# Graph kernel with two gather layers: four row buffers instead of two, eight index buffers, and loops of more chunks

## What is computed

```
# layer 0
deg  = segment_sum(1, dst);  norm = rsqrt(deg[src]) * rsqrt(deg[dst])
x    = layernorm(x + segment_sum(x[src] * norm, dst))
# layer 1
h    = relu(edge_feat @ W1 + b1);  w = (h @ W2 + b2).reshape(e, 4, 8, 8)
m0   = ALPHA * ((s[src] * sh0) . w_000 + C110 * (v[src] * sh1) . w_110)
m1   = ALPHA * (s[src] . w_011 * sh1 + (v[src] * sh0) . w_101)
x    = layernorm(x + segment_sum([m0, m1], dst) + SI_SCALE * x @ si)
```

## Time and profile before

| | us |
|---|---|
| median of 3 executions (5684.65 to 5692.03) | 5685.9 |
| span of the profiled execution | 5691.5 |
| POOL busy in it | 3201.0 |
| DVE busy in it | 3000.7 |
| PE busy in it | 2619.5 |

### The profile page before, as it was taken

The page is one execution under the profiler, slowest core; times in us unless marked ns, Lnnn a source line. Parts: engine busy times, 40 slices in busy tenths (PEclk is TensorE's granted clock), DMA queues, the critical chain, the costliest instruction groups (busy, mean ns, idle before and its releaser), DMA issues. The chain is left out here.

```text
span 5691.5 us, 47787 instructions
## 1 busy us (share of the span) xinstructions
PE 2619.5 (46%) x12834; PEld 1908.4 (34%) x12834; DVE 3000.7 (53%) x4177; ACT 325.3 (6%) x556; POOL 3201.0 (56%) x3341
## 2 busy tenths in 40 slices
PE   8981111111111111111257666666666666666662
PEld 8981111111111111111234444444444444444441
DVE  5561000000000100000169999999999999999994
ACT  0000000000000000000011111111111111111110
POOL 0006666666666666666455555656565656555550
PEclk9997555555555555555567787878787878778785
DMA  0000000000000000000011111111111111111110
GB/s 21 0 11 12 12 12 12 12 12 12 12 12 12 12 12 12 12 12 12 13 25 23 23 21 23 21 23 21 23 21 23 21 23 21 23 21 23 21 22 12
DMA packets 169134, 95.17 MB, mean 17 GB/s; under 512 B 100154, under 2 KB 153915, under 8 KB 168920
## 3 DMA queue, kind: packets, MB, share of 16 engines
q0 software_dynamic: 106496, 54.74, 6.6%
q1 hardware_dynamic: 62620, 40.21, 2.6%
HBM read 89.90 MB, written 4.81 MB: 17 GB/s over the span
## 5 line engine op out<-in xcount | busy, mean ns | idle before, releaser
L282 POOL DMA_INDIRECT xg<-x_table,idx x1664 | 1570.2, 944 | 1156.2 <-DVE feat L695 602.5
L282 POOL DMA_INDIRECT xg<-scaled_x_table,idx x1664 | 1625.8, 977 | 771.8 <-issue 579.1
L572 DVE TENSOR_TENSOR sumT<-sumT,ps 32x64 f32 x832 | 172.6, 207 | 2281.6 <-remote 1876.9
L383 PE MATMUL ps<-oh,xg 128*32 128x64 f32 x3328 | 378.0, 310 | 2029.5 <-DMA xg<-scaled_x_table,idx 2016.8
L452 PE MATMUL ps<-w,hT 128*128 128x256 f32 x3328 | 979.4, 445 | 482.9 <-DVE prod L711 428.4
L720 DVE TENSOR_REDUCE red<-prod 128x192 f32<-128x1536 f32 x416 | 1201.0, 2905 | 0.0
L383 PEld LDWEIGHTS ps<-oh,xg 128*32 128x32 f32 x3328 | 347.8, 172 | 2059.8 <-issue 2059.2
L452 PEld LDWEIGHTS ps<-w,hT 128*128 128x128 f32 x3328 | 688.6, 218 | 971.3 <-DVE prod L711 715.8
L383 PE MATMUL ps<-oh,msg 128*32 128x64 f32 x3328 | 370.1, 310 | 398.9 <-DVE msg L732 388.0
L383 PEld LDWEIGHTS ps<-oh,msg 128*32 128x32 f32 x3328 | 347.3, 172 | 467.4 <-issue 467.4
L445 PE MATMUL ps<-efT,w 128*64 128x512 f32 x832 | 490.9, 674 | 5.1 <-ACT x_sb L318 5.1
(11 more groups left out here) (71 smaller groups left out, 598.1 us busy)
## 6 DMA issues: line engine op xcount, KB each, us to landing
xg<-scaled_x_table,idx POOLq DMA_INDIRECT x1664
efT<-in_efT SPq DMA_DIRECT2D x104, 256.0 KB, 2.5
xg<-x_table,idx POOLq DMA_INDIRECT x1664
idx<-in_src SPq DMA_DIRECT2D x208, 8.0 KB
sh<-in_sh SPq DMA_DIRECT2D x104, 32.0 KB, 2.3
x_sb<-in_x SPq DMA_DIRECT2D x1, 1568.0 KB
scaled_x_table<-z_sb SPq DMA_DIRECT2D x1, 1568.0 KB
x_table<-q_sb SPq DMA_DIRECT2D x8, 196.0 KB
```

The lines of the kernel that those rows point to most:

```text
L282: pool.indirect_dma_start(xg[k][:, t, :], None, table, bass.IndirectOffsetOnAxis(ap=idx[k][:, t:t + 1], axis=0),).then_inc(s_g[layer][GPC ...
L383: mm = pe.matmul(ps_sum[:, k, j, :], rows[:, TPG * j + t, :], oh[k][:, TPG * j + t, :], start=(t == 0), stop=(t == TPG - 1))
L572: dve.tensor_tensor(sumT[:, bass.ds(base, WIN)], sumT[:, bass.ds(base, WIN)], ps_sum[:, k, j, :], ALU.add).then_inc(s_acc[layer], 1)
```

## The change

Four row buffers `xg` and eight index buffers `idx`. A row buffer has one semaphore per layer, counting all 16 DMAs of a chunk, instead of four. One set of eight index semaphores serves both layers. POOL may fill a row buffer for chunk n once chunk n-4 has been used. POOL's and SP's loops take eight chunks an iteration, and the first eight chunks stand ahead of them; ACT's loop, PE's loop of layer 0 and DVE's loop of layer 1 take four. The waits for the tables stand once ahead of each layer. SP loads the first two chunks' edge features ahead of its layer 0 loop, and in layer 1 loads chunk n's indices just ahead of chunk n's edge features. `part_i` is placed in the storage of `prod`. PE's loop of layer 1, DVE's loop of layer 0, the one-hots, the PSUM areas and the edge-feature buffers stay as they were.

```diff
@@ -43,8 +43,9 @@
     CPP = NC // PIECES
     PW = CPP * D
     BPP = PW // P
-    PAIRS = CHUNKS // 2
-    assert CHUNKS % 2 == 0 and n_out + WIN <= SUMW and PW == 512
+    QUADS = CHUNKS // 4
+    OCTS = CHUNKS // 8
+    assert CHUNKS % 8 == 0 and n_out + WIN <= SUMW and PW == 512
     ctx = ExitStack()
     with ctx:
...
@@ -97,8 +97,8 @@
         near = sb("near", [P, 1], I32)
-        idx = [sb(f"idx{k}", [P, TPC], I32) for k in range(2)]
-        xg = [sb(f"xg{k}", [P, TPC, D]) for k in range(2)]
+        idx = [sb(f"idx{m}", [P, TPC], I32) for m in range(8)]
+        xg = [sb(f"xg{k}", [P, TPC, D]) for k in range(4)]
         sh = [sb(f"sh{k}", [P, TPC, 4]) for k in range(2)]
         efT = [sb(f"efT{k}", [P, TPG * P]) for k in range(2)]
         oh = [sb(f"oh{k}", [P, TPC, WIN]) for k in range(2)]
...
@@ -107,11 +107,13 @@
-        prod = [sb(f"prod{b}", [P, TPG, 6, MUL, MUL]) for b in range(2)]
+        prod_all = sb("prod_all", [P, 2, TPG, 6, MUL, MUL])
+        prod = [prod_all[:, b] for b in range(2)]
+        part_i = prod_all[:].rearrange("p b t c i o -> p (b t c i o)")[:, 0:TILES].bitcast(I32)
...
@@ -140,10 +142,10 @@
         s_root = sem("s_root")
         s_w2x = sem("s_w2x")
         s_table = [sem("s_y_table"), sem("s_x1_table")]
-        s_idx = [[sem(f"s_idx{l}_{k}") for k in range(2)] for l in range(2)]
+        s_idx = [sem(f"s_idx{m}") for m in range(8)]
+        s_edge = [sem(f"s_edge{k}") for k in range(2)]
         s_begun = [sem(f"s_begun{l}") for l in range(2)]
-        s_edge = [sem(f"s_edge{k}") for k in range(2)]
-        s_g = [[sem(f"s_g{l}_{q}") for q in range(2 * GPC)] for l in range(2)]
+        s_g = [[sem(f"s_g{l}_{k}") for k in range(4)] for l in range(2)]
         s_oh = [sem(f"s_oh{l}") for l in range(2)]
         s_sum = [sem(f"s_sum{l}") for l in range(2)]
         s_acc = [sem(f"s_acc{l}") for l in range(2)]
...
@@ -190,51 +192,47 @@
             sp.dma_start(si[:], si_d).then_inc(s_win, 16)
-            for k in range(2):
-                sp.dma_start(idx[k][:], src_d[k]).then_inc(s_idx[0][k], 16)
+            for m in range(8):
+                sp.dma_start(idx[m][:], src_d[m]).then_inc(s_idx[m], 16)
             sp.wait_ge(s_scaled, 1)
             sp.dma_start(y_d.rearrange("(p c) f -> p c f", c=NC), z_sb[0:NP, :, :]).then_inc(s_table[0], 16)
-
-            def load_indices(layer, n, k, after):
-
-                for j in range(GPC):
-                    sp.wait_ge(s_g[layer][GPC * k + j], after)
-                sp.dma_start(idx[k][:], src_d[n]).then_inc(s_idx[layer][k], 16)
             def load_edges(n, k):
                 sp.dma_start(efT[k][:], efT_d[n]).then_inc(s_edge[k], 16)
                 sp.dma_start(sh[k][:], sh_d[n]).then_inc(s_edge[k], 16)
-            with sp.Fori(1, PAIRS) as i:
-                for k in range(2):
-                    load_indices(0, 2 * i + k, k, 16 * TPG * i)
+            def reload_indices(layer, n, m, landed):
+                sp.wait_ge(s_g[layer][m % 4], landed)
+                sp.dma_start(idx[m][:], src_d[n]).then_inc(s_idx[m], 16)
             for k in range(2):
                 load_edges(k, k)
-                for j in range(GPC):
-                    sp.wait_ge(s_g[0][GPC * k + j], 16 * TPG * PAIRS)
-                sp.dma_start(idx[k][:], src_d[k]).then_inc(s_idx[1][k], 16)
+            with sp.Fori(1, OCTS) as i:
+                for m in range(8):
+                    reload_indices(0, 8 * i + m, m, 512 * i - 256 + 256 * (m // 4))
+            for m in range(8):
+                reload_indices(0, m, m, 256 * (CHUNKS // 4) - 256 + 256 * (m // 4))
             x1_v = x1_d.rearrange("(p c) f -> p c f", c=NC)
             for q in range(PIECES):
                 sp.wait_ge(s_row[0], q + 1)
                 sp.dma_start(x1_v[:, q * CPP:(q + 1) * CPP, :], node_cols(q_sb, q)).then_inc(s_table[1], 16)
-            def reload_edges(i, k):
-
-                sp.wait_ge(s_msg, 3 * (2 * i + k - 1))
-                load_edges(2 * i + k, k)
-
-
-            load_indices(1, 2, 0, 16 * TPG)
-            with sp.Fori(1, PAIRS - 1) as i:
-                load_indices(1, 2 * i + 1, 1, 16 * TPG * i)
-                reload_edges(i, 0)
-                load_indices(1, 2 * i + 2, 0, 16 * TPG * i + 16 * TPG)
-                reload_edges(i, 1)
-            load_indices(1, CHUNKS - 1, 1, 16 * TPG * (PAIRS - 1))
-            for k in range(2):
-                reload_edges(PAIRS - 1, k)
+            def reload_edges(n, k):
+
+                sp.wait_ge(s_msg, 3 * (n - 1))
+                load_edges(n, k)
+
+            reload_edges(2, 0)
+            reload_edges(3, 1)
+            reload_edges(4, 0)
+            reload_edges(5, 1)
+            reload_edges(6, 0)
+            reload_edges(7, 1)
+            with sp.Fori(1, OCTS) as i:
+                for m in range(8):
+                    reload_indices(1, 8 * i + m, m, 512 * i - 256 + 256 * (m // 4))
+                    reload_edges(8 * i + m, m % 2)
             full = n_out // NC
...
@@ -271,30 +269,33 @@
             pool.wait_ge(s_offsets, 2)
             pool.partition_all_reduce(spans[:], span[:], P, RMAX).then_inc(s_span, 1)
-            def gather(layer, k, table, i, rows_used):
-                pool.wait_ge(s_idx[layer][k], 16 * i + 16)
-                for used, count in rows_used:
+            def gather(layer, m, table, loaded, uses):
+
+                k = m % 4
+                pool.wait_ge(s_idx[m], loaded)
+                for used, count in uses:
                     pool.wait_ge(used, count)
-
-                pool.wait_ge(s_table[layer], 16 * (1 if layer == 0 else PIECES))
                 pool.sem_inc(s_begun[layer], 1)
                 for t in range(TPC):
                     pool.indirect_dma_start(
                         xg[k][:, t, :], None, table,
-                        bass.IndirectOffsetOnAxis(ap=idx[k][:, t:t + 1], axis=0),
-                    ).then_inc(s_g[layer][GPC * k + t // TPG], 16)
-
-            for k in range(2):
-                gather(0, k, y_d, 0, [])
-            with pool.Fori(1, PAIRS) as i:
-                for k in range(2):
-                    gather(0, k, y_d, i, [(s_sum[0], 2 * i + k - 1)])
-            for k in range(2):
-
-                gather(1, k, x1_d, 0, [(s_sum[0], CHUNKS)])
-            with pool.Fori(1, PAIRS) as i:
-                for k in range(2):
-                    gather(1, k, x1_d, i, [(s_ft, 4 * (2 * i + k - 1)), (s_scal, 2 * i + k - 1)])
+                        bass.IndirectOffsetOnAxis(ap=idx[m][:, t:t + 1], axis=0),
+                    ).then_inc(s_g[layer][k], 16)
+
+            pool.wait_ge(s_table[0], 16)
+            for m in range(8):
+                gather(0, m, y_d, 16, [(s_sum[0], m - 3)] if m >= 4 else [])
+            with pool.Fori(1, OCTS) as i:
+                for m in range(8):
+                    gather(0, m, y_d, 16 * i + 16, [(s_sum[0], 8 * i + m - 3)])
+            pool.wait_ge(s_sum[0], CHUNKS)
+            pool.wait_ge(s_table[1], 16 * PIECES)
+            for m in range(8):
+                gather(1, m, x1_d, 16 * OCTS + 16, [(s_ft, 4 * (m - 3)), (s_scal, m - 3)] if m >= 4 else [])
+            with pool.Fori(1, OCTS) as i:
+                for m in range(8):
+                    gather(1, m, x1_d, 16 * i + (16 * OCTS + 16),
+                           [(s_ft, 4 * (8 * i + m - 3)), (s_scal, 8 * i + m - 3)])
         @block.scalar
         def _(act):
...
@@ -327,24 +328,23 @@
                     act.wait_ge(s_w, g - 1)
                 act.activation(hT[b][0:HID, :], ps_h[b][0:HID, :], ACT.Relu, bias=b1[:]).then_inc(s_relu, 1)
-            def scalars(n, k, landed, first):
-                for j in range(GPC):
-                    act.wait_ge(s_g[1][GPC * k + j], landed)
+            def scalars(n, k, b, landed, first):
+                act.wait_ge(s_g[1][b], landed)
                 if not first:
                     act.wait_ge(s_red, GPC * (n - 1))
-                act.activation(feat[k][:, :, MUL:2 * MUL], xg[k][:, :, 0:MUL], ACT.Copy).then_inc(s_scal, 1)
-
-            for k in range(2):
+                act.activation(feat[k][:, :, MUL:2 * MUL], xg[b][:, :, 0:MUL], ACT.Copy).then_inc(s_scal, 1)
+
+            for m in range(4):
                 for j in range(GPC):
-                    rectify(GPC * k + j, j % 2, k == 0 and j < 2)
+                    rectify(GPC * m + j, j % 2, m == 0 and j < 2)
                     if j == 0:
-                        scalars(k, k, 16 * TPG, True)
-            with act.Fori(1, PAIRS) as i:
-                for k in range(2):
+                        scalars(m, m % 2, m, 16 * TPC, m < 2)
+            with act.Fori(1, QUADS) as i:
+                for m in range(4):
                     for j in range(GPC):
-                        rectify(2 * GPC * i + GPC * k + j, j % 2, False)
+                        rectify(4 * GPC * i + GPC * m + j, j % 2, False)
                         if j == 0:
```

(48 more changed lines are left out.)

12 lines of the change are left out of this document (6 added, 6 removed).

## The result

The changed kernel takes 5818.28 us (median of 4 executions, 5817.99 to 5819.17) against 5685.27 us for the kernel before: ratio 1.0231, 95% interval 1.0216 to 1.0245. It is **slower by 2.3%**, where the prediction said 5471 us and a range of 5400 to 5620.

A forecast was written before the change was run, and what follows sets the result against it. The prediction took POOL to bound layer 0 and DVE layer 1. From the 5691.5 us span, -245 + 15 + 15 = -215, less 5.6 us to reach the median, gave 5471 us, range 5400 to 5620.

The forecast's parts named there:

- Four row buffers, layer 0: Layer 0: POOL's wait moves to chunk n-4's sum, removing 245 us of 252.6 us waiting; bounds 0 and 252.6.
- the 5 us are owed per 32 DMAs whatever the program says: Layer 0: POOL's pauses come with every 32 DMAs, so nothing moves: 5686 us; no-change chance 0.02.
- Counts pass only when the stream stops: Layer 0: late counts arrive only when POOL's gathers pause; 30 pauses instead of 51, about 5612 us; chance 0.18.
- Start of layer 1: POOL streams on for about eight chunks and late PE counts hold DVE; 15 us more, bounds 0 and 60.
- Longer loops: DVE's loop body, two chunks made four, may fetch code at returns; 15 us more, bounds 0 and 58.
- The second rival: DVE fetches code at every return: 58 us instead of 15, 5514 us; with two fetches 116, 5572; chance 0.15.
- What stays in layer 0: Layer 0: 44.7 us of POOL's DMAs stretched while DVE makes one-hots; no gain counted, bounds 0 and 44.7.
- Index loads, table waits, single semaphores: Both layers: extra loads hidden, steady phase the same, dropped waits gain nothing; 16 us at most.
- "slower" rival: Layer 1: late counts delay DVE in each of 104 chunks; at 10 us, +139 us, 5825 us; chance 0.06.
- three signs that would make it wrong: Pauses of 5 us return; DVE idling 1 us each fourth chunk; DVE awaiting PE past layer 1's first chunks.

The follow-up runs named there:

- e3: Changed kernel, but layer 1's first eight gathers wait as before the change (chunk n for chunk n-2's features); 5761.29 us.
- e4: Kernel before, with only DVE's layer 1 loop taking four chunks an iteration instead of two; 5743.2 us against 5685.82, ratio 1.0099.
- e9: Changed kernel with layer 1 put back to two row buffers and two-chunk loops on DVE and ACT; ratio 1.0002 to the kernel before.
- e10: Kernel before with 64 one-number memsets on DVE in each chunk of layer 0; 5734.57 us against 5706.25, ratio 1.0051.
- e5: Kernel before with two tiny memsets on POOL behind each gather of layer 0; 5752.82 us against 5711.53, ratio 1.0069.
- e1: Changed kernel with half of layer 0's window matmuls left out, gathers, one-hots and adds kept; 5795.07 us.

## Why the prediction was wrong, point by point

- **Four row buffers, layer 0: -245 forecast, -8.5 measured** (2384.0 to 2375.5, within the scatter of the same code). This is the step that failed. It took the lateness of a count as a fixed delay of at most 20.3 us that older counts would cover, "then all 252.6 us go". The lateness is a backlog, and more slack only lets POOL build a bigger one. The sentence "what is late next is POOL's own issue: 1664 x 1.248" left out that nothing had shown the gathers going through at 1.248 for longer than a pair of chunks. The rows had it: 32 gathers and 5 us, each time, over 2384 us, with few exceptions. The rival "the 5 us are owed per 32 DMAs whatever the program says" was the right one for this layer. I gave it 0.02, because of one stretch without a pause; but that stretch ended in a pause of 6.0 us as well, after 48 gathers.
- **Counts pass only when the stream stops (0.18)** had the mechanism half right and its size wrong: it let POOL stream four chunks and then rest 5 us. The rest is 9.7.
- **Start of layer 1: +15 forecast, bounds 0 and 60, measured +58.5.** The mechanism was right, and e3 shows it. Mis-sized: the value stood near the lower end while the rows spoke for the upper one. The stream had 80 gathers (100 us), not eight chunks, because chunk 5 waits for chunk 1's features.
- **Longer loops: +15 forecast, bounds 0 and 58, measured 62.7 alone (e4) and 72.1 with the rest of the change.** The second rival, with its 2.3 us a return, was right in kind and in the price of a return (2.5). It missed the 15 us that the adds and products lose behind it. I had chosen 15 because no return stalled in the trace before; with the body half as long none did.
- By the rule of the Trainium skill (Runtime: NRT & Kernel Launch, "Instruction fetch mechanics") a taken branch stalls for a fetch if its target lies outside the current two pages of 256 instructions. The runs agree that a return can cost a fetch: 2.5 us and five packets on DVE, nothing on POOL (e9). They do not show where the limit lies. I had written that POOL's body of some 290 would stall too; two pages are 512, so that was a misreading. But my count of some 440 for DVE's body is under 512 as well, and it stalls. Five packets of 8 KB an iteration would be some 640 instructions by the 16 KB that the Trainium skill gives there for 256, an estimate; so my count may be too low.
- **What stays in layer 0: 0 forecast, and it stayed.** POOL's DMA rows in the layer took 1625.8 us before and 1622.3 after. That the one-hots of line 559 are a two-port operation, which the rule cited there needs, no run shows; the trace shows only that the stretched DMAs stand beside them.
- **Index loads, table waits, single semaphores: 0 forecast**, and e9 agrees for them together (ratio 1.0002).
- **The "slower" rival** (0.06) gave 5825 us and is closest to the measured time, but by another way: DVE's steady wait for PE in layer 1 did not grow by a microsecond a chunk.
- Of the three signs that would make it wrong, two came: pauses back every few chunks, and 1 us or more at each fourth chunk on DVE. The third, DVE waiting for PE beyond layer 1's first chunks, did not: its two long waits (68.7 and 17.6 us) are both in chunk 0.

## What to carry to other kernels

If an engine pauses by the same few microseconds at each N-th item, first ask whether the pause is owed for the items: divide it by N, and look what a longer run does. A rate limit looks like a late signal, and no number of buffers cures it; here more buffers let the fast engine run further ahead and held up a neighbour where it hurt, at the start of the next stage. Unroll a loop on the engine that sets the pace only after weighing its body: here the same work in a body twice as long lost 2.5 us at each return.

## What was not expected of the hardware

- Gathers with 64 and with 128 rows cost nearly the same, 1.42 and 1.42 to 1.44 us each in the long run, and more than the 1.248 us that POOL takes to issue them.
- Memsets of one number on an idle DVE, waited for by nobody, made the kernel 0.5% slower (e10), and two on POOL that fit between its gathers 0.7% (e5).
- The Trainium skill (NOTIFIC — the notification-queue block, "7.1 Overflow: three behaviours, one of which stalls the engine") says that the block which writes trace records pushes back on its producers when its internal buffers are full. Prices for each instruction of every engine, and PE held in the middle of a chunk, would fit that. No run here shows it: every time in this case comes with a recorded profile, so whether the limit is there without one was not tried.
- TensorE's granted clock in layer 0 was 0.55 of full speed before and 0.56 after, near the level of 1.2 GHz, and full speed (2.4 GHz) with half of the matmuls in e1:

```profile
424.00:2781.00 2357.00, 196.68 (x1648) 172.39 (x1648) 218.12 (x517) 0.00 (x0) 1625.57 (x1664) 1.00 0.08 12
```

The layer was hardly shorter for it, so PE's speed is hardly a bound there. A version that beats both kernels was not found; e9 ties with the kernel before.
